# New per-engine orders of work, with orders of their own for the first and last chunks, and LayerNorm normalisations moved from VectorE to ScalarE

## The reference, cut to what matters

```python
xz = x @ in_proj_w.T;  x_inner, z = split(xz)            # 512 and 512 columns
x_conv = silu(conv1d_causal(x_inner, taps=4) + conv_b)
dt, B_ssm, C_ssm = parts of x_conv @ x_proj_w.T           # dt through softplus
h = exp(dt*A) * h + (dt*x_conv) * B_ssm                   # 512 channels x 16 states, along the tokens
y = sum over states of h*C_ssm + x_conv*D
mamba = (y * silu(z)) @ out_proj_w.T
...
for each of 2 layers:                                     # 8 heads of 64, windows of 128 tokens
    q, k, v = split(shift_token(x) @ wqkv); q, k = rotary(l2norm(q)), rotary(l2norm(k))
    x = x + local_attention(q, k, v) @ wo
    h = layernorm(shift_token(x)) * lg + lb
    a, g = split(h @ w1 + b1);  x = x + (a * gelu(g)) @ w2 + b2
```

## Time and profile before

| | |
|---|---|
| median of 3 runs | 2378.99 us (2377.95 to 2399.59) |
| profiled execution, its own time | 2396.66 us |
| its span, first to last instruction | 2394.9 us |
| instructions | 37640 |
| mean granted TensorE clock | 0.957 of full speed |

### The profile page before, as it was taken

The page is one execution under the profiler, slowest core; times in us unless marked ns, Lnnn a source line. Parts: engine busy times, 40 slices in busy tenths (PEclk is TensorE's granted clock), DMA queues, the critical chain, the costliest instruction groups (busy, mean ns, idle before and its releaser), DMA issues. The chain is left out here.

```text
span 2394.9 us, 37640 instructions
## 1 busy us (share of the span) xinstructions
PE 2111.3 (88%) x10944; PEld 1346.1 (56%) x10944; DVE 2070.7 (86%) x2948; ACT 1602.0 (67%) x3895; POOL 895.7 (37%) x1038
## 2 busy tenths in 40 slices
PE   6589898998899989899888998889889898998788
PEld 2355565655556556565555645655556655656456
DVE  2889898998889988899888989889888998899983
ACT  3666676767666766668667676776766666777662
POOL 1343333343433433244333343334342433333430
PEclk9799999999999999999999999999999999999899
DMA  3467675677666766667756776657765677666762
GB/s 120 119 160 200 161 186 139 155 191 188 145 171 146 188 186 147 157 166 174 188 133 169 185 166 176 142 159 197 170 152 135 166 198 165 183 163 150 186 151 56
DMA packets 113130, 388.52 MB, mean 162 GB/s; under 512 B 11408, under 2 KB 32272, under 8 KB 94368
## 3 DMA queue, kind: packets, MB, share of 16 engines
q0 software_dynamic: 46080, 151.02, 35.6%
q1 hardware_dynamic: 66848, 235.10, 29.6%
HBM read 238.75 MB, written 155.71 MB: 165 GB/s over the span
## 5 line engine op out<-in xcount | busy, mean ns | idle before, releaser
L614 DVE TENSOR_TENSOR_SCAN hb<-dA,state,hb 128x512 f32<-128x512 f32 x512 | 672.9, 1314 | 14.8 <-ACT dA L843 3.1
L1044 POOL DMA_DIRECT2D ysum<-dA x256 | 223.9, 892 | 556.6 <-DVE dA L621 507.0
L1028 POOL COPY state<-hb 128x2 f32<-128x2 f32 x256 | 209.7, 819 | 560.5 <-DVE hb L614 560.4
L843 ACT ACTIVATE dA<-dt_sb,amat 128x512 f32<-128x512 f32 x512 | 349.0, 721 | 98.4 <-DMA ysum<-dA 97.0
L949 ACT ACTIVATE probs<-ring,nmax 128x256 f32<-128x256 f32 x512 | 235.9, 478 | 227.0 <-DVE nmax L719 226.8
L1308 PE MATMUL ring<-hT,w 128*128 128x256 f32 (+1 forms) x1536 | 347.9, 382 | 6.6 <-ACT hT L970 6.5
L1308 PEld LDWEIGHTS ring<-hT,w 128*128 128x128 f32 (+1 forms) x1536 | 268.2, 178 | 83.3 <-issue 24.4
L924 ACT ACTIVATE rot<-rot,rnorm 128x64 f32<-128x64 f32 x1024 | 256.4, 339 | 82.7 <-POOL rnorm L1109 80.5
L621 DVE TENSOR_TENSOR dA<-hb,bc 128x1024 f32<-128x1024 f32 x256 | 310.8, 1214 | 0.0
L607 DVE TENSOR_TENSOR hb<-u_sb,bc 128x1024 f32<-128x1024 f32 x256 | 307.4, 1201 | 1.2 <-DMA bc<-bc_rows 1.2
L1109 POOL TENSOR_TENSOR rnorm<-rnorm,powers 128x8 f32<-128x8 f32 x128 | 235.3, 1838 | 23.5 <-POOL rnorm L1106 23.5
(11 more groups left out here) (118 smaller groups left out, 3464.7 us busy)
## 6 DMA issues: line engine op xcount, KB each, us to landing
bc<-bc_rows SPq DMA_DIRECT2D x128, 1024.0 KB, 5.9
ysum<-dA POOLq DMA_DIRECT2D x256, 512.0 KB, 7.0
wqkv<-in_wqkv SPq DMA_DIRECT2D x48, 512.0 KB, 8.3
w<-in_w SPq DMA_DIRECT2D x16, 1364.0 KB, 13.9
w<-in_w SPq DMA_DIRECT2D x16, 768.0 KB, 6.8
tab<-in_tab SPq DMA_DIRECT2D x64, 128.0 KB, 7.3
ysum<-xconv POOLq DMA_DIRECT2D x32, 256.0 KB, 4.2
wo<-in_wo SPq DMA_DIRECT2D x16, 512.0 KB, 11.9
```

The lines of the kernel that those rows point to most:

```text
L614: dve.tensor_tensor_scan(hb[:, k % H_RING, :], dA[:, k % DA_RING, :], hb[:, k % H_RING, :], state[:, k:k + 1], ALU.mult, ALU.add).then_inc ...
L843: act.activation(dA[:, k % DA_RING, :], dt_sb[:, j, :], ACT.Exp, scale=amat[:, n:n + 1]).then_inc(dA_ready.sem, 1)
```

## The change

Three things are changed together.

First, the tables. Each engine has three strings, `..._FIRST` for the pass that starts chunk 0 (with the `+` parts of chunk 1), `..._ORDER` for six passes, and `..._LAST` for the last pass, which finishes chunks 6 and 7. All have been written anew. There are 8 passes in place of 10. The PSUM banks are handed out in the new order of TensorE's groups.

```diff
-        for c in range(-AHEAD, CHUNKS):
-            run_pass(DVE_ORDER, of_chunk, c)
+        for order, c in passes_of(DVE_FIRST, DVE_ORDER, DVE_LAST):
+            run_pass(order, of_chunk, c)
...
+def passes_of(first, steady, last):
+
+    return [(first, 0), *((steady, c) for c in range(CHUNKS - 2)), (last, CHUNKS - 2)]
```

```diff
+                dve.wait_ge(*mv_ready.at(it, 2 * h + 2))
+                part = slice(2 * h, 2 * h + 2)
+                dve.tensor_scalar(mv[:, part, 0], mv[:, part, 0], -1.0, None, ALU.mult).then_inc(negated.sem, 1)
...
+                dve.wait_ge(*mv2_ready.at(it, 2 * f + 2))
+                dve.tensor_scalar(mv2[:, :, 0], mv2[:, :, 0], -1.0, None, ALU.mult).then_inc(negated2.sem, 1)
...
+                pool.wait_ge(*rstd2_ready.at(it, f + 1))
+                pool.sem_inc(passed, 1)
+                pool.tensor_tensor(shift2[:, :], mv2[:, :, 0], rstd2[:, :], ALU.mult)\
+                    .then_inc(shift2_ready.sem, 1)
...
-                        dve.tensor_scalar(hn[:, v, ft * P:(ft + 1) * P], src, mv2[:, v, 0:1], rstd2[:, v:v + 1],
-                                          ALU.subtract, ALU.mult).then_inc(hn_ready.sem, 1)
+            def normalized(out, w):
+                return act.activation(out, xtok[:, w, :], ACT.Identity, bias=shift1[:, w:w + 1],
+                                      scale=rstd[:, w:w + 1])
...
+            def normalize(f):
+                l, half = divmod(f, 2)
+                act.wait_ge(*shift2_ready.at(it, f + 1))
+                act.wait_ge(*hid_ready.at(it, NH * f))
+                act.wait_ge(*filled(it, ("sh", f)))
...
+                        act.activation(hn[:, v, ft * P:(ft + 1) * P], src, ACT.Identity, bias=shift2[:, v:v + 1],
+                                       scale=rstd2[:, v:v + 1]).then_inc(hn_ready.sem, 1)
```

Third, one wait is added to SP's `y`, so that the sum may land in `xin` only once the next chunk's halo has been saved:

```diff
                     sp.wait_ge(*filled(min(it + 1, CHUNKS - 1), ("conv", j)))
+                    sp.sem_inc(passed, 1)
+                    sp.wait_ge(*halo_saved.at(min(it + 1, CHUNKS - 1), 1))
                     sp.sem_inc(passed, 1)
                     sp.wait_ge(*gated.at(it - 1, j + 1))
```

More of the change, by code:

```diff
@@ L78 @@
[L78 to L86, removed]
+heads(7) o(6,3) s(7,0) s(7,1) +q(0) pT(7,0) pT(7,1) +k(0) pT(7,2) pT(7,3) o(7,0) o(7,1) rb(7) o(7,2) o(7,3)
+wo(6) +v(0) wo(7) +heads(0) sh(3) +q(1) +s(0,0) +s(0,1) +k(1) +dt(2) +pT(0,0) hT(3) out(0) +dt(3) h(3,0)
@@ L92 @@
[L92 to L96, removed]
@@ new lines @@
+e(5,2) e(5,3) v(5) rb(4) dA q(6) dA k(6) pT(5,0) pT(5,1) pT(5,2) pT(5,3) +softplus(0) rb(5) turn(q,6)
+turn(k,6) last(2) heads(6) v(6) dA dA dA dA e(6,0) e(6,1) hn(2) e(6,2) pT(6,0) e(6,3) q(7) pT(6,1) hT(2)
+pT(6,2) k(7) turn(q,7) h(2,0) h(2,1) dA dA pT(6,3) h(2,2) h(2,3) h(2,4) h(2,5) dA dA +dA +dA turn(k,7)
++skip(0) rb(6)
+"""
+POOL_FIRST = """
+halo norm(0) norm(1) q(0) turn(q,0) turn(k,0) +norm(0) scan scan q(1) add(0) add(1) turn(q,1) turn(k,1) scan
+skip(0) scan scan q(2) add(2) add(3) add(4) scan turn(q,2) turn(k,2) add(5) scan scan add(6) +norm(1) scan
@@ new lines @@
+scan q(3) add(7) add(8) turn(q,3) turn(k,3) add(9) stats(0) carry scan add(10) scan add(11) tail scan scan
+q(4) add(12) add(13) scan +halo add(14) scan scan add(15) add(16) scan add(17) turn(q,4) turn(k,4) skip(1)
+scan stats(1) scan q(5) add(18) add(19) scan +tail add(20) turn(q,5) turn(k,5) scan merge(0) add(21) q(6)
+add(22) scan scan scan add(23) add(24) scan scan add(25) add(26) turn(q,6) turn(k,6) stats(2) q(7) scan scan
+add(27) turn(q,7) add(28) add(29) scan scan turn(k,7) carry2 +q(0)
@@ new lines @@
++pT(6,2) +pT(6,3) +turn(q,7) +turn(k,7) +h(2,0) +h(2,1) +rb(6) +h(2,2) +h(2,3) +dA +heads(7) +dA +dA +dA
++v(7) +h(2,4) +h(2,5) +e(7,0) +last(2) +e(7,1) +e(7,2) +e(7,3) +pT(7,0) +pT(7,1) +pT(7,2) +pT(7,3) +rb(7)
++hn(3) +hT(3) +h(3,0) +last(3) +h(3,1) +h(3,2) +h(3,3) +h(3,4) +h(3,5)
+"""
+POOL_LAST = """
+scan add(30) +scan add(31) +add(0) +turn(q,0) +turn(k,0) +q(1) +scan merge(1) +add(1) stats(3) +turn(q,1)
++scan +skip(0) +scan +add(2) +add(3) +turn(k,1) +scan +scan +q(2) +add(4) +add(5) +add(6) +scan +turn(q,2)
@@ L387, in build @@
+    passes = [(c + later, name) for order, c in passes_of(PE_FIRST, PE_ORDER, PE_LAST)
+              for later, name in groups_of(order)]
     at = {group_: n for n, group_ in enumerate(passes)}
@@ L1143, in _ @@
         of_chunk = [stages(c) for c in range(CHUNKS)]
-        for c in range(-AHEAD, CHUNKS):
-            run_pass(POOL_ORDER, of_chunk, c)
+        for order, c in passes_of(POOL_FIRST, POOL_ORDER, POOL_LAST):
+            run_pass(order, of_chunk, c)
     @block.tensor
@@ L1350, in _ @@
         of_chunk = [stages(c) for c in range(CHUNKS)]
-        for c in range(-AHEAD, CHUNKS):
-            run_pass(PE_ORDER, of_chunk, c)
+        for order, c in passes_of(PE_FIRST, PE_ORDER, PE_LAST):
+            run_pass(order, of_chunk, c)
     ctx.close()
```

370 lines of the change are left out of this document (245 added, 125 removed).

## The result

| | before | changed |
|---|---|---|
| median | 2378.91 us (2377.95 to 2399.59, 4 runs) | 2245.98 us (2240.71 to 2253.13, 4 runs) |
| profiled execution, its span | 2394.9 us | 2238.9 us (time 2240.71) |
| mean granted TensorE clock | 0.957 | 0.976 |

The ratio is 0.942, with a 95% interval of 0.937 to 0.948: 5.8% faster, where the forecast was 4.7% (2268 us). The profiled execution of the changed kernel is its fastest of four, 0.2% under its median, and that of the kernel before was 0.7% over its median. So the spans and cycles of the two traces show 156 us of gain (6.5%) where the medians show 133; differences between traces are to be read with that in mind.

What follows compares the result with a forecast made beforehand. TensorE (88% busy) and VectorE (86%) were taken to share the bound. Start 56.7 + first chunk 258.0 + 6 x 275.5 + last chunk and tail 315.3 = 2283.0 us of span, scaled to 2268 us; range 2185 to 2352.

Steps and rivals of the forecast that it cites:

- three waits: VectorE's waits for `ysum`, `xtok` and the output transfer: 14.4 us a chunk if all go, bounds nothing and all.
- Start and ends: Start kept at 56.7 us (3 us later, cancelled by a gain), first chunk 258.0, last chunk and tail 315.3.
- The middle value: Cycle of the six middle chunks: 275.5 us, taken midway between 265.0 (VectorE's side) and 286.5 (TensorE's side).
- The upper end: Cycle from TensorE's side, where only its weight and gate waits go: 286.5 us.
- The clock: TensorE in six chunks: fewer pauses return part of up to 11 us a chunk stretched by half clock.
- The split of the gain: Of about 83 us from the six chunks' cycle, 47 from normalisations gone, the rest from waits.
- ScalarE and GpSimd: Added work: ScalarE 93 us for 192 activations, GpSimd (POOL) at most 53 us for 48 multiplies.
- A: Rival: TensorE's side rules, its ScalarE waits stay, cycle 286.5 us, time 2350 us; chance 0.15.
- D: Rival: transfer waits only change place, cycle 286 to 291 us, time within 1% of before; chance 0.08.
- B: Rival: VectorE's side rules, TensorE's pauses vanish, cycle 265.0 us, time 2190 us; chance 0.12.
- C: Rival: ScalarE stands in its queue ahead of `hn` and `start`, cycle 296 us, time 2421 us; chance 0.07.
- The halo's wait: Added wait on `halo_saved` in SP's queue: costs nothing while the halo is saved a long way ahead.

Runs made afterwards that it cites:

- xn_alone: Kernel before with SP's three places moved and only `xn` and `start` on ScalarE, `hn` staying on VectorE: 2284.61 us, ratio 0.953.
- act_old_orders: Kernel before, old tables, with the normalisations moved to ScalarE, each `hn` right ahead of its `hT`: 2419.21 us, ratio 1.013.
- sp_and_act: Kernel before, old engine tables, with SP's three places moved and the normalisations on ScalarE: 2316.80 us, ratio 0.970.
- no_ends: Changed kernel with its middle tables for all chunks, no own orders for first and last chunks: 2250.12 us, ratio 0.942.
- dve_new_orders: Changed kernel with its new tables but the normalisations back on VectorE: 2292.43 us, ratio 0.960.
- sp_places: Kernel before with only three words of SP's table moved, `y(1)`, `x(0)` and `y(0)` each ahead of a `bc`: 2279.57 us, ratio 0.956.
- y_alone: Kernel before with only `y(1)` and `y(0)` moved in SP's table, `x(0)` left behind `bc(4)`: 2314.07 us, ratio 0.969.
- stats1_early: Changed kernel with one word of GpSimd's middle table moved, `stats(1)` ahead of `tail`: 2241.93 us, ratio 0.939.

## Why the prediction was right, point by point

The forecast was 4.7% and 5.8% came. Two of the three waits it named went, VectorE's work became less and the clock rose, as it said. But the value of the cycle was a middle taken between two ends and not a reading, so that it came near is in part luck. The shares it gave to the causes were wrong.

**Start and ends.** Forecast 56.7, 258.0 and 315.3; measured 62.3, 245.7 and 318.6. The start got 5.6 us longer where 3 and a cancelling gain were expected. Other runs split it: with the old orders or the middle tables and the normalisations on ScalarE the first scan comes at 58.3 to 58.9 us (xn_alone, act_old_orders, sp_and_act, no_ends), with the own first orders and the normalisations on VectorE at 61.5 (dve_new_orders). Before it was 56.7. So the own first orders cost 3.6 to 4.8 us and the move 0.8 to 2.2; `q(0)` ahead of `dt` is only one part of these orders. The first chunk gives back more than that: 308.0 together against 314.7. Last chunk and tail together gave 8.9 us and not 12.2; the tail kept its length.

**The transfers.** "If all three waits go, that is the 14.4 us a chunk": sp_places gave 14.4 a chunk, but with two of the three waits gone (11.0) and the third still there (3.1); the rest came from other waits and the clock. So the waits for the moved transfers counted whole or more (by y_alone, 10.9 us a chunk for the 6.9 of `ysum`, then 3.5 for the 4.1 of `xtok`), where the middle value had counted about half. That the number is the same is chance.

**The middle value.** This is the term that was mis-sized: "I take the middle, 275.5 us" between 265.0 and 286.5, measured 268.7, 83% of the way to VectorE's end. The upper end took TensorE's waits for ScalarE as standing by themselves. The one for `probs` did not: in sp_places, where ScalarE's work was untouched, it fell from 30.4 us to 8.9, so most of it was VectorE's wait handed on. The one for `rot` did stand by itself there (30.2 and 33.4 us), and fell to 3.7 under the new tables only. The clock helped as argued: TensorE's busy time in six chunks fell by 43.2 us, 7.2 a chunk, of the 11 a chunk which I had put as its upper bound.

**The split of the gain.** I gave 47 of 83 us in the six chunks to the normalisations and the rest to waits. The runs say it the other way round: of 20.7 us a chunk, SP's places gave 14.4, and the move with the new tables 6.3 (taken in the other order, 17.0 and 3.7). The 7.8 a chunk for the normalisations is right for the move under the new tables (7.9 by the traces of dve_new_orders and changed, some 6.3 scaled to their medians), wrong for the move as such (it costs 2.6 to 3.3 under the old ones). My sum had no place for a value that depends on the tables.

**ScalarE and GpSimd.** Forecast +93 and up to +53, measured +78.9 and +32.5. The pieces of `hn` took 467 ns on average and not 450, those of `xn` and `start` 590 and not 558; by their means the 192 are 97.6 us. But neighbours overlap: at 1012.20 us one piece takes 0.49 us and the next starts 0.40 us after it. The 128 of `hn` keep ScalarE busy for 50.3 us and the 64 others for 34.1, together 84.4. The sum of 93 had counted the overlaps twice. On VectorE likewise: the four rows that I added to 74.2 us are 42.9 and 23.5 with the overlaps taken once, 66.4, so less was taken off it than I said. The negations took 0.18 us, not 0.25, and VectorE's -62 was -53.9. Some 6 us on each engine are left that I have not followed.

The Trainium skill, "ScalarE: Activation LUTs", section "What ACT_TABLE_LOAD costs", which I cited for 186 ns plus 0.833 ns a column plus 93 ns an operand, gives 479 and 585 ns. The trace agrees within 3% for the pieces that read from SBUF (489 and 590) and is 7% below it for those of `hn` that read from PSUM (445).

**The rivals.** A's 286.5 did not come, nor did D's waits that "change their place"; B's condition, that TensorE's pauses vanish and the clock with them, came nearly (idle 13.7 us a chunk, clock 0.99), and so did its value. C's test was ScalarE idle over 10 us a chunk ahead of L993 and L968; it was 9.6 (43.0 + 9.7 + 5.1 by six), and a third of it lay in slack, as stats1_early showed. But C was nearer than the time tells: two GpSimd instructions more or less in each chain were 1.3%, by a way that stays open.

**The halo's wait** cost nothing visible: VectorE waits for no `ysum` in the six chunks.

## What to carry to other kernels

When an engine waits for a transfer, look at what stands ahead of that transfer in its queue, and at whom that one waits for: three words in SP's table, which took `y` and `x` out from behind a `bc` that VectorE itself had to release, gave 4.4%, more than moving 192 instructions did. Work taken off a bound engine is worth its time only if the engine that gets it reaches it in time: the same move lost 1.3 to 1.5% under tables that put it right ahead of its reader, and gained 1.8% under tables with other stages between. Before adding up the edits of a change, ask which of them need each other.
